# The projection of a decoder layer, with convolution taps over two batches in one operation

## The reference

```python
z = rmsnorm(u, pre_norm_w) @ in_proj_w.T            # 256 -> 768 channels
zc = z.transpose(0, 2, 1)
z_pre = conv(zc, short_w, K=3, causal, per channel) + short_b
x2, x1, v = split(z_pre, 3)
xv = x1 * v                                         # goes into the long convolution
y = (longconv(xv) + xv * D_skip) * x2
```

## Time and profile before

| | us |
|---|---|
| device time, three runs | 2273.16, 2278.83, 2898.13 |
| median | 2278.83 |
| span of the profiled execution, first to last instruction | 2275.8 |
| of it, up to the first instruction of `longconv` | 219.95 |
| PE, DVE, ACT, POOL busy in the span | 2026.0, 1494.9, 1174.4, 889.2 |

### The profile page before, as it was taken

How to read it: one execution, slowest core, us unless ns; L and a number is a source line. 1 busy time by engine, 2 the same in 40 slices (tenths; PEclk the granted TensorE clock), 3 DMA queues, 4 the chain that set the end, 5 groups by cost and what they waited for, 6 DMA issues and landing times. The chain is left out here.

```text
span 2275.8 us, 39720 instructions
## 1 busy us (share of the span) xinstructions
PE 2026.0 (89%) x12960; PEld 1411.1 (62%) x12960; DVE 1494.9 (66%) x2701; ACT 1174.4 (52%) x2313; POOL 889.2 (39%) x1308
## 2 busy tenths in 40 slices
PE   6786959999999948999999999999999999978998
PEld 4665847888888834565556655565556655534554
DVE  6897444444444417777777777877777777734776
ACT  6774234444444422555555555555555555554554
POOL 3444625555555421343333333343333333332232
PEclk9998979999999968999999999999999999988999
DMA  3344011222212234324433344324433344011222
GB/s 112 131 137 156 2 64 48 75 74 74 74 69 70 74 93 101 78 64 101 100 85 89 67 99 106 84 69 96 100 86 92 65 99 100 25 60 47 92 74 74
DMA packets 104638, 188.04 MB, mean 83 GB/s; under 512 B 27816, under 2 KB 77992, under 8 KB 98344
## 3 DMA queue, kind: packets, MB, share of 16 engines
q1 hardware_dynamic: 104488, 186.14, 30.3%
HBM read 110.23 MB, written 58.79 MB: 74 GB/s over the span
## 5 line engine op out<-in xcount | busy, mean ns | idle before, releaser
L1704 DVE TENSOR_REDUCE at_mneg<-at_ps_s 128x1 f32<-128x384 f32 (+3 forms) x704 | 437.8, 635 | 112.8 <-PE at_ps_s L1345 112.2
L1476 ACT ACTIVATE at_pt<-at_ps_w 128x512 f32<-128x512 f32 x640 | 375.1, 596 | 242.3 <-PE at_ps_w L1356 241.9
L1559 POOL TENSOR_SCALAR_AFFINE_SELECT at_pt<-at_pt 128x256 f32<-128x256 f32 (+1 forms) x640 | 230.7, 365 | 590.5 <-ACT at_pt L1476 588.3
L1344 PE MATMUL at_ps_s<-at_ks,at_qs 96*128 96x128 bf16 (+3 forms) x1024 | 259.1, 306 | 43.6 <-DVE at_mneg L1704 30.5
L1356 PE MATMUL at_ps_w<-at_qs,at_ks 97*128 97x512 bf16 (+3 forms) x1024 | 243.4, 300 | 5.3 <-ACT at_pt L1476 4.6
L1344 PEld LDWEIGHTS at_ps_s<-at_ks,at_qs 96*128 96x128 bf16 x1024 | 87.3, 99 | 235.4 <-DVE at_mneg L1704 136.3
L879 POOL TENSOR_TENSOR ml_m_lo<-ml_m,ml_m_hi 128x512 fp32r<-128x512 f32 x96 | 135.5, 1418 | 196.2 <-ACT ml_m_hi L794 196.0
L1372 PE MATMUL at_ps_o<-at_pt,at_val 128*32 128x512 f32 (+3 forms) x2048 | 166.0, 442 | 9.2 <-POOL at_pt L1559 9.1
L1345 PE MATMUL at_ps_s<-at_mask,at_ident 128*128 128x128 bf16 (+2 forms) x704 | 173.5, 246 | 0.0
L819 ACT ACTIVATE ml_gl<-ml_ps_g 128x512 f32<-128x512 f32 x96 | 56.6, 589 | 167.1 <-PE ml_ps_u L127 163.3
L1515 POOL TENSOR_TENSOR at_parts<-at_rest,at_parts 128x512 bf16<-128x512 f32 x64 | 74.4, 1163 | 158.7 <-ACT at_parts L1457 158.7
(11 more groups left out here) (248 smaller groups left out, 5579.3 us busy)
## 6 DMA issues: line engine op xcount, KB each, us to landing
parts_d<-at_parts SPq DMA_DIRECT2D x64, 384.0 KB, 2.5
at_ks<-parts_d SPq DMA_DIRECT2D x192, 128.0 KB, 7.2
at_qs<-parts_d SPq DMA_DIRECT2D x32, 384.0 KB, 5.0
pj_xin<-in_x SPq DMA_DIRECT2D x16, 512.0 KB, 5.1
gate_d<-pj_zc SPq DMA_DIRECT2D x16, 512.0 KB, 2.6
xv_all<-pj_turned_xv SPq DMA_DIRECT2D x16, 512.0 KB, 4.0
ml_turned_y<-xv_all SPq DMA_DIRECT2D x16, 512.0 KB, 3.5
ml_x<-gate_d SPq DMA_DIRECT2D x16, 512.0 KB, 4.2
```

Of the source, the lines that this page charges most:

```text
L1344: pe.matmul(out[:, i, :], qs[par][0:ROWS, h, toks], ks[par][0:ROWS, h, 0:(qt + 1) * P], start=i == 0, stop=False)
L1476: act.activation(pt[u % RING][:], ps_w[u % 2][:], ACT.Exp, scale=SCALE).then_inc(exped, 1)
L1559: pool.affine_select(out=diag, in_=diag, compare_op=ALU.is_ge, fill=0.0, base=0, pattern=pattern, channel_multiplier=-1).then_inc(cut, 1)
L1704: dve.tensor_reduce(mneg[:, g, h0 % HG:h0 % HG + count, qt], view_score(ps_s[s % 2], qt, count), AX_X, ALU.max, negate=True).then_inc(maxe ...
```

## The change

`project` works in eight pairs p of two batches. All loops on the engines are gone: every step is written out.

- `zc`, `xv`, `side`, `x_hi`, `x_lo` get a dimension of two batches. `zc` is one buffer for a pair in place of two for a batch, `xv` likewise; `x_hi` and `x_lo` stay double, by pairs.
- A PSUM tile is two banks, one for each batch; there are three such tiles (BANKS), taken in rotation.
- Taps on ACT and DVE, the product on POOL and the side addition handle 2 x 512 columns in one operation.
- SIDES = [4, 5]: for both tiles of x2 tap 1 goes over ACT and POOL. DVE adds tap 0 behind the side copy, POOL adds the side tile after that.
- The steps of squares, root, norm, turn, high and low stay per batch, two of each in a pair.
- SP's order in a step is both loads of the next pair, filter rows (seven per step, from p = 3), both places, both stores of x2. The stores wait for the side additions.

```diff
-    SIDE = 4
-    DONE = [1, 2, 3, 4, 6, 5]
+    SIDES = [4, 5]
+    BANKS = 3
+    NPAIR = B // 2
...
-        ps_z = [n.psum(f"ps_z{i}", [P, T]) for i in range(CT)]
+        ps_z = [n.psum(f"ps_z{i}", [P, 2, T]) for i in range(BANKS)]
...
+            def store_gate(p):
+                sp.wait_ge(side_added, len(SIDES) * (p + 1))
+                for j in range(2):
+                    sp.dma_start(x2_d[2 * p + j:2 * p + j + 1].rearrange("o p k t -> (o p) k t"), zc[:, 0:KT, j, :]).then_inc(x2_stored, 16)
+
+            def place(b):
+                sp.wait_ge(chunked, 2 * KT * (b // 2) + KT * 2 - 1 + b % 2)
+                sp.dma_start(xv_all[:, b:b + 1].rearrange("p o g n -> p (o g n)"),
+                             turned_xv[b % 2][:].rearrange("p g n -> p (g n)")).then_inc(placed[b % 2], 16)
...
+            for p in range(NPAIR):
+                if p + 1 < NPAIR:
+                    load(2 * p + 2)
+                    load(2 * p + 3)
+                if p == 2:
+                    store_filters()
+                if p == 3:
+                    sp.wait_ge(f.filt_out, 16 * KT)
+                if p >= 3:
+                    place_filters(7 * (p - 3), min(C, 7 * (p - 2)))
+                place(2 * p)
+                place(2 * p + 1)
+                store_gate(p)
...
         def _(act):
+            for p in range(NPAIR):
+                more = p + 1 < NPAIR
+                if more:
+                    squares(2 * p + 2)
                 for k, ct in enumerate(ORDER):
+                    bank = ps_z[(CT * p + k) % BANKS]
+                    act.wait_ge(z_ready, CT * p + k + 1)
...
+                    act.activation(zc[:, ct], bank[:], ACT.Identity, bias=tb[:, ct:ct + 1],
                                    scale=tap[:, ct, 2:3]).then_inc(tap2_done, 1)
+                    if k in SIDES:
+                        i = SIDES.index(k)
+                        wait(act, side_added, len(SIDES) * (p - 1) + i + 1)
+                        act.activation(side[i][:], bank[:], ACT.Copy, scale=tap[:, ct, 1:2]).then_inc(side_set, 1)
+                    if more and k == 0:
+                        norm(2 * p + 2)
+                    if more and k == 1:
+                        squares(2 * p + 3)
+                    if more and k == 2:
+                        high(2 * p + 2)
+                        norm(2 * p + 3)
+                    if more and k == 4:
+                        high(2 * p + 3)
+                    if k in (2, 5) and 2 * p + k // 4 < 3:
+                        exponents(2 * p + k // 4)
...
         def _(pool):
+            for p in range(NPAIR):
+                if p + 1 < NPAIR:
+                    root(2 * p + 2)
+                    root(2 * p + 3)
+                gate(p, 0)
+                if p < 2:
+                    prepare_filters(2 * p)
+                gate(p, 1)
+                add_side(p, 0)
+                add_side(p, 1)
...
         def _(pe):
+            turn(0)
+            turn(1)
             pe.wait_ge(w_split, 1)
+            for p in range(NPAIR):
+                par = p % 2
                 for k, ct in enumerate(ORDER):
                     cols = slice(ct * P, (ct + 1) * P)
+                    past = CT * p + k - BANKS
+                    if past >= 0:
+                        pe.wait_ge(tap0_done, past + 1)
+                    for j in range(2):
+                        if k == 0:
+                            pe.wait_ge(low_set, 2 * p + j + 1)
+                        mm = products3(pe, ps_z[(CT * p + k) % BANKS][:, j, :], ...)
+                    mm.then_inc(z_ready, 1)
+                    if p + 1 < NPAIR and k in (1, 3):
+                        turn(2 * p + 2 + k // 2)
...
         def _(dve):
+            for p in range(NPAIR):
+                more = p + 1 < NPAIR
+                for k, ct in enumerate(ORDER):
+                    bank = ps_z[(CT * p + k) % BANKS]
+                    dve.wait_ge(tap2_done, CT * p + k + 1)
+                    if k in direct:
+                        dve.scalar_tensor_tensor(zc[:, ct, :, 1:T], bank[:, :, 0:T - 1], ...).then_inc(tap1_done, 1)
+                        dve.wait_ge(tap1_done, len(direct) * p + direct.index(k) + 1)
+                    else:
+                        dve.wait_ge(side_set, len(SIDES) * p + SIDES.index(k) + 1)
+                    dve.scalar_tensor_tensor(zc[:, ct, :, 2:T], bank[:, :, 0:T - 2], ...).then_inc(tap0_done, 1)
+                    if more and k == 2:
+                        low(2 * p + 2)
+                    if more and k == 4:
+                        low(2 * p + 3)
+                    if k == 3:
+                        chunk(p, 0)
+                chunk(p, 1)
```

More of the change, by code:

```diff
@@ L362, in exponents @@
                     act.activation(f.readout[:], f.readout[:], ACT.Exp).then_inc(f.exp_out, 1)
-            squares(0, 0)
-            norm(0, 0)
-            high(0, 0)
+            for b in range(2):
+                squares(b)
+                norm(b)
+                high(b)
             act.wait_ge(par_loaded, 64)
[L369 to L372, removed]
+            for p in range(NPAIR):
+                more = p + 1 < NPAIR
+                if more:
+                    squares(2 * p + 2)
@@ L373, in step @@
                 for k, ct in enumerate(ORDER):
[L374 removed]
+                    bank = ps_z[(CT * p + k) % BANKS]
+                    act.wait_ge(z_ready, CT * p + k + 1)
                     if ct < KT:
[L377 removed]
+                        wait(act, x2_stored, 32 * p)
                     else:
[L379 to L380 removed]
+                        wait(act, gated, KT * (p - 1) + k // 2 + 1)
@@ L444, in _, with turn @@
             pe.wait_ge(par_loaded, 64)
-            def turn(b, par):
+            def turn(b):
                 pe.wait_ge(normed, QT * (b + 1))
@@ L491, in _ @@
             dve.tensor_tensor(w_lo[:], w_raw[:], w_hi[:].bitcast(F32), ALU.subtract).then_inc(w_split, 1)
[L492 to L516, removed]
-                    if k == 3 and not last:
-                        low(b + 1, 1 - par)
-                chunk(0)
-                chunk(1)
-                dve.wait_ge(side_added, b + 1)
-                tap0(ORDER[SIDE])
-                if isinstance(b, int) and b == 3:
@@ new lines, in _, with chunk @@
+            low(0)
+            low(1)
+            def chunk(p, k):
+                if k == 0:
+                    for i in range(2):
+                        wait(dve, placed[i], 16 * p)
+                dve.wait_ge(gated, KT * p + k + 1)
+                for j in range(2):
+                    dst = turned_xv[j][:, k * C:(k + 1) * C, :].rearrange("p c n -> p n c")
+                    dve.transpose(dst, xv[:, k, j, :].rearrange("p (n c) -> p n c", c=C)).then_inc(chunked, 1)
+            direct = [k for k in range(CT) if k not in SIDES]
```

119 lines of the change are left out of this document (48 added, 71 removed).

## The result

The changed kernel takes **2365.76 us** (median of four runs, 2359.0 to 2368.96) against 2276.04 us for the kernel before beside it: a ratio of 1.0396, 95% interval 1.0376 to 1.0417. It is 3.96% slower, 15.8 us above the 2350 forecast and inside the range of 2328 to 2372. One of the four runs of the kernel before took 2898.13 us; the ratios here are of the fast runs alone. The profiled execution has a span of 2363.9 us.

What follows compares the result with a forecast made beforehand. VectorE's taps bound the stage before; after, late loads do. Start 50.1, six rings 219.0 and last pair 20.6 total 289.7 against 218.0: +71.7 on 2275.8, plus 3.0, gives 2350 us; range 2328 to 2372.

Steps and rivals of the forecast that it cites:

- The ring: In project, the next pair's load waits behind the stores and last side addition; a pair takes 36.5 us against 23.3.
- Durations of the wide operations: Operations on 1024 elements: ACT tap 1.21 us, side copy 1.13, DVE tap 1.27, POOL addition 2.4.
- Three in four: Chance that PE's clock drops at the 2.3 us gap before a pair's second turn; pair ends at 37.0 us, kept 35.25.
- The high end of the range: Load landing at 7.6 us and clock always dropped: 6 x 38.7 + 70.7 = 303, +85 us, 2364.
- The end: Last pair of project: last addition ends at 17.6 us, second store lands 2.6 after its issue, 20.6 in all.
- Throughput: By engine work alone a pair would take 19.1 us instead of 23.3; DVE's saving would not reach the end.
- Signs: Expected in the profile: squares idle 8 to 10 us, PE about 12, clock 0.5, second gap near 2, DVE under 60%.
- 2307 to 2327: Rival of a shorter ring, 30 to 33 us, through earlier engine starts or a kept clock: +28 to +48; chance 0.12.
- The loads are hidden: Rival: last addition comes earlier or loads pass it, so 23.2 us per ring, 2275 to 2292, no change; chance 0.10.
- The two-turn chain alone eats the saving: Within the hidden-loads rival: squares, root, norm and two turns per pair still take 23.2 us, 24.9 with the clock dropped.
- Throughput is reached: Rival: all waits overlap and a pair takes 19.1 us, -34 us, 2245; chance 0.03.
- the 16 us less: By the skill page's 3.2 us per 512 KB transfer, each ring would be 2.7 us shorter and the sum 16 us less.

Runs made afterwards that it cites:

- the last experiment: Changed kernel with loads ahead, turns reordered, and next pair's first squares, root and norm prepared one pair ahead: 2246.78 us, ratio 0.9868 to the kernel before.

## Why the prediction was right

**Sign, mechanism and place** held. The ring is where it was put, its steps come in the order of the walk, and the loads' move takes away most of it. Term by term:

- **Durations of the wide operations.** ACT's tap 1.20 us (1.21 forecast), side copy 1.12 (1.13), DVE's tap 1.28 (1.27), POOL's addition 2.38 to 2.41 (2.4). Adding the price of 512 more elements, taken from other rows of the same engine, was good to 0.01 us on ACT and DVE.
- **Pair 0** ended at 51.06, 50.1 forecast.
- **The ring**, 38.7 against 36.5, is the mis-sized term: 13.2 of the 16.6 us missed in the stage. "Two stores and the load take 0.35 of issue each, load at 0.8" was too small: the stores took 0.81 each and the load left at 1.76. It took the store's 0.35 for the load too, whose row shows 0.59. The landing took 6.35 from there, 5.9 forecast. So the turn starts at 13.1 instead of 11.75 and the second one at 24.0 instead of 22.3. Tile 4 comes 5.46 us after the second turn, the dropped clock's 5.5, and the ring closes at 38.6. "Three in four" for that drop was near: the clock fell behind five of the six second gaps, in or right behind the turn, and these rings are 38.5 to 40.1; the sixth is 36.4. The high end of the range was worked out with 38.7 per ring, and that is what came, but by luck: its load lands at 8.4 (here 8.1) and its clock always falls, while here the rings with the dropped clock average 39.2 and one ring kept it.
- **The end.** From pair 6's last addition to the next stage 24.96 us against 20.6 + 1.95 (218.0 to 219.95). The last addition came 17.4 on, 17.6 forecast. But the gate stores landed after 4.4 us instead of the 2.6 of the earlier trace rows. They leave right behind two placements now and read rows in two pieces; which of these counts was not tried. The transfers end at 305.5 us, after a last half microsecond at 369 GB/s, and the next stage starts 2.7 later.
- **Throughput** was the step that mattered least and it was right: nothing that DVE saves shows.
- **Signs.** The squares idle some 12 us on the load, not 8 to 10, as the load lands later than forecast; PE's 13 us, the clock of 0.50, the second gap of 2.4 us and DVE at 50% came as listed.
- **A sum that is wrong.** By the prediction's own terms a ring of 30 us gives 70.7 + 6 x 30 - 218.0 = +33 and one of 33 us +51, so 2312 to 2330, and not 2307 to 2327. Nothing else in it rests on that.

**The rivals.** "The loads are hidden" had a price of 2275 to 2292. The load did wait, so the rival fell. But its price assumed that hiding the load is all it takes, and the loads ahead alone gave 2309: the walk of that rival let the squares and the root pass straight on, and left out POOL's order, in which the root stands behind the last side addition. With the root moved (2283) or the turns reordered (2281) the total is as that rival has it, 2275 to 2292. "The two-turn chain alone eats the saving" fits the first: a ring of 24.7, with the second turn waiting for the low part. In the second the order of the turns is another and that wait is gone; there PE waits for the norm, and the norm for POOL's root. "Throughput is reached", 19.1 us a pair, is what the last experiment shows, at 19.4.

**Where the 89.7 us lie.** Load order 57, POOL's root 26 more once the load is out of the way; or load order 57 and the order of the turns 28 more; the clock takes 12 inside these. The parts overlap, since the root and the turns stand on the same path, so they are not to be added up.

The Trainium skill, DMA: Bandwidth & Descriptors, "Rules for kernel authors", asks to issue a transfer early and wait late, and the trace agrees: the same transfers, issued a pair earlier, cost nothing and 57 us came back. Its section "Anatomy of one DMA" gives its figure for transfers that GpSimd issues, which the prediction did not say; these are issued by SyncE. That figure, by an estimate 3.2 us for 512 KB, is not reached here: the loads landed after 6.6 us behind four transfers and after 4.1 in a quiet queue. So the 16 us less that the prediction worked out by the page would have led away from the result.

**Open.** How much of the 1.3% of the last kernel the narrow operations would have had from the same order was not tried; before, DVE was busy for 21.5 of the 23.3 us of two batches. So order alone could have given at most 1.8 of the 3.9 us a pair, and the rest, below 21.5, needs DVE's smaller work. Which of its edits beyond loads and turns gives how much was not separated either. Nor was it tried to issue the loads from another engine than the stores, which would take them out of the one queue.

## What to carry to other kernels

When steps are merged into wider ones, everything that used to be one step ahead must be moved one wide step ahead, on every in-order queue it passes: here the load behind SyncE's stores, and then the root behind GpSimd's last addition. Ask of each transfer and each small operation of preparation what stands ahead of it in its queue, and what that waits for; a saving of busy time is worth nothing until the wait is gone. When one wait is taken away, walk the ring again before pricing the gain, because the next one on the path stands close behind.

## What the runs showed of the hardware

- **The issue of a transfer is not a fixed cost.** SyncE's load took 0.60 us behind one gate store and one placement (median, kernel before, 0.43 to 0.67), 1.15 us behind two of each in the kernel after, and 0.376 us (median) with the loads ahead, where most had waited for their buffer first; right behind filter rows they took 0.73 to 0.77 there. In the last kernel it took 0.37 us when issued 3.7 us after two gate stores, with transfers still moving 399 GB/s over 72 to 73. The gate store took 0.35 us in the kernel before and in the one with its loads late, and 0.57 to 1.23 wherever the buffer holds two batches side by side, so that a batch's row is in two pieces of 2 KB. Whether the pieces or the transfers ahead make it longer was not tried.
- **Landing goes with what is ahead in the queue**: the same 512 KB load landed after 4.1 us in a quiet queue, 5.1 behind one store and one placement, 6.6 behind two of each (medians).
- **A gap of 2.0 to 2.7 us on TensorE may or may not cost the clock.** The 2.38 us before 228.56 had a granted clock of 0.50 behind it; the 2.38 us before 182.76 in the kernel with the extra matmuls had 1.00. Ahead of the first, TensorE had idled 13 us, run at 0.50 over 218 to 221 and at 1.00 over 222 to 226; ahead of the second it had 1.00 in every stretch looked at from 152 us on. In the kernel after alone, with nearly the same run-up each time, the clock fell behind five such gaps and stayed at 1.00 behind the sixth. In the kernel before, 2.03 us dropped it and 2.67 did not the earlier trace rows, so the length of the gap alone does not tell; what does was not found.
